# Six shared chunks instead of seven ahead of the routed experts, and the weights' low halves on POOL

## The reference

```python
x = x + 0.5 * ffn(layernorm(x))          # layer half 0
x = x + attention(layernorm(x))
x = x + 0.5 * ffn(layernorm(x))          # layer half 1, same weights

def ffn(h):                              # 8 routed experts, F = 512, the best 2 of 8 per token
    probs = softmax(h @ gate_W.T)
    gates = the two largest of probs, 0 for the others
    out_e = (silu(h @ w1_e[e]) * (h @ w3_e[e])) @ w2_e[e]
    routed = sum over e of gates[e] * out_e
    shared = (silu(h @ w1_s) * (h @ w3_s)) @ w2_s / 8     # 8 shared parts of 64, together 512 wide
    return 0.5 * shared + 0.5 * routed

def attention(a):                        # linear: exp(k) weights, cumulative sums over the sequence
    q, k, v = split(rms_norm(a) @ w_qkv.T)
    w = exp(rms_norm(k))
    y = sigmoid(rms_norm(q)) * cumsum(w * v) / (cumsum(w) + 1e-6)
    u, g = split(y @ w_swiglu.T)
    return a + (u * silu(g)) @ w_out.T
```

## Time and profile before

| what | value |
|---|---|
| median of 3 runs | 734.16 us (734.12 to 734.52) |
| span of the profiled execution | 733.5 us, 0.7 us below the median |
| PE busy | 660.3 us, 90% of the span |
| DVE busy | 458.8 us, 63% |
| ACT busy | 411.3 us, 56% |
| POOL busy | 430.6 us, 59% |
| routed stage of half 0 | 112.4 to 302.1 us |
| attention's first DVE instruction | 313.1 us |

### The profile page before, as it was taken

The page is one execution under the profiler, slowest core; times in us unless marked ns, Lnnn a source line. Parts: engine busy times, 40 slices in busy tenths (PEclk is TensorE's granted clock), DMA queues, the critical chain, the costliest instruction groups (busy, mean ns, idle before and its releaser), DMA issues.

```text
span 733.5 us, 14294 instructions
## 1 busy us (share of the span) xinstructions
PE 660.3 (90%) x4860; PEld 602.1 (82%) x4860; DVE 458.8 (63%) x1177; ACT 411.3 (56%) x861; POOL 430.6 (59%) x511
## 2 busy tenths in 40 slices
PE   3878999999999999957987777999999999999995
PEld 3767879999999999825654574888999999999983
DVE  6678895554445555359999867884555555544536
ACT  2658617666666666236654436664666666666520
POOL 5600075777777776489987424007577777777530
PEclk9989999999999999989999997999999999999999
DMA  9542011221222231131100002402212212212137
GB/s 296 231 78 40 1 42 38 56 52 52 52 55 52 52 53 44 57 105 44 47 12 1 0 1 46 73 2 49 40 55 54 52 52 56 51 53 52 43 104 261
DMA packets 35685, 45.91 MB, mean 63 GB/s; under 512 B 6432, under 2 KB 27936, under 8 KB 35232
## 3 DMA queue, kind: packets, MB, share of 16 engines
q1 hardware_dynamic: 25632, 24.39, 11.8%
q0 software_dynamic: 9984, 20.63, 11.5%
HBM read 28.41 MB, written 16.58 MB: 61 GB/s over the span
## 4 chain that ended last, share of the span: by engine, by line
PE 65%; DVE 20%; issue 4%; ACT 4%; POOL 3%; DMA 2%; SPq 1%; ACTq 0%; POOLq 0%; DVEq 0%
PE psY L1487 18%; PE psG L1334 6%; PE psU L1336 6%; PE psG L1336 6%; PE psU L1335 6%; PE psG L1335 6%; PE psU L1334 6%; PE psH L1405 4%; DVE rec L1076 3%; PE psT L1433 2%; DVE hs L748 2%; DVE XN L738 2%; DVE ln_stats L725 1%; DVE xn L1060 1%; POOL results L641 1%
## 5 line engine op out<-in xcount | busy, mean ns | idle before, releaser
L626 POOL DMA_INDIRECT rows<-tokens,source x156 | 153.7, 985 | 156.3 <-DVE source L900 98.6
L1155 ACT ACTIVATE silu<-psG 128x512 f32<-128x512 f32 x220 | 131.1, 596 | 150.6 <-PE psG L1336 147.2
L954 DVE TENSOR_TENSOR hT<-silu,psU 128x512 f32<-128x512 f32 x156 | 107.4, 688 | 158.9 <-PE psU L1336 150.3
L641 POOL DMA_INDIRECT results<-yout,target x156 | 153.8, 986 | 63.3 <-issue 45.7
L1487 PE MATMUL psY<-W,hT 128*128 x1232 | 162.4, 275 | 1.8 <-DVE yout L980 1.8
L1487 PEld LDWEIGHTS psY<-W,hT 128*128 128x128 f32 x1232 | 150.4, 191 | 2.2 <-DVE hT L954 2.2
L1229 ACT ACTIVATE w_high<-W13H 128x1024 fp32r x78 | 82.7, 1061 | 59.0 <-PE psU L1336 54.8
L1334 PE MATMUL psG<-xTH,w_high 128*128 128x256 f32 x312 | 100.0, 321 | 0.7 <-ACT w_low L1229 0.7
L1336 PE MATMUL psG<-xTH,w_low 128*128 128x256 f32 x312 | 88.0, 282 | 0.0
L1336 PE MATMUL psU<-xTH,w_low 128*128 128x256 f32 x312 | 88.0, 282 | 0.0
L1335 PE MATMUL psU<-xTL,w_high 128*128 128x256 f32 x312 | 87.7, 281 | 0.0
(11 more groups left out here) (188 smaller groups left out, 1215.7 us busy)
## 6 DMA issues: line engine op xcount, KB each, us to landing
W<-w_e SPq DMA_DIRECT2D x3, 2048.0 KB, 13.7
tokens<-XN SPq DMA_DIRECT2D x16, 260.0 KB, 5.9
Y<-results SPq DMA_DIRECT2D x32, 128.0 KB, 2.2
YF<-results SPq DMA_DIRECT2D x16, 256.0 KB, 5.9
rows<-tokens,source POOLq DMA_INDIRECT x156
results<-yout,target POOLq DMA_INDIRECT x156, 2.3
X<-x SPq DMA_DIRECT2D x8, 256.0 KB, 5.5
out<-X SPq DMA_DIRECT2D x8, 256.0 KB, 2.8
```

The costliest lines, as they stand in the source:

```text
L626: pool.indirect_dma_start(rows[:, slot(l, g), t, :], None, tokens, bass.IndirectOffsetOnAxis(ap=source[:, tile:tile + 1], axis=0))\
L641: pool.indirect_dma_start(results, bass.IndirectOffsetOnAxis(ap=target[:, tile:tile + 1], axis=0), yout[:, g % 2, t, :], None).then_inc(y_ ...
L954: dve.tensor_tensor(hT[:, s.u // PT % 2, half, :].rearrange("p f c -> p (f c)"), silu[:, s.u % 2, :], psU[:, s.u % 2, :], ALU.mult).then_i ...
L1155: act.activation(silu[:, s.u % 2, :], psG[:, s.u % 2, :], ACT.Silu).then_inc(silu_done, 1)
```

## The change

Two constants change: `FRONT` is [6, 6], and the seventh chunk (number 6) is `LATE_CHUNK`. Its four steps, its `out_shared` and its `add_shared` stand behind the routed stage in both halves; in half 1 they did so before. Its hidden values go to `hs_late`, a tile of its own that lies over the routing's `at_place`, `in_tile` and `pair`, since `Y` covers the half of `hs` that it had. The 8 `low_part` calls leave DVE's queue. POOL makes them right behind the tokens' low parts, ahead of its wait for the tables and the first `fetch_row`, each as soon as ACT has made its high piece. DVE's copy of the first group of rows (`copy_xT`) and PE's turning of it follow `FRONT` and stand four steps earlier.

```diff
-FRONT = [7, 6]
+FRONT = [6, 6]
+LATE_CHUNK = 6
...
         memory = overlaid(
+            [("below_late", [P, 2 * FT * CH * P], fp32), ("hs_late", [P, FT, CH * P], fp32)],
             [("Y", [P, 4, TOPK, TB, D], fp32), ("XNT", [P, NT], fp32)],
...
 # POOL, behind low_xnT and low_shared
+                def low_part(j):
+                    w, cols = j % 2, bass.ds(j // 2 * WCOLS, WCOLS)
+                    pool.wait_ge(high_made, j + 1)
+                    pool.tensor_tensor(W13L[:, w, cols], W13[:, w, cols], W13H[:, w, cols].bitcast(fp32),
+                                       ALU.subtract).then_inc(w_split, 1)
+                if l == 0:
+                    for j in range(2 * WPARTS):
+                        low_part(j)
                 pool.wait_ge(tokens_out, 16 * CHUNKS * (l + 1))
...
 # DVE
-                    gated(hs[:, s.u // FT, s.u % FT, :], s, shared_at(l, s.i))
+                    home = hs_late if s.i // FT == LATE_CHUNK else hs[:, s.u // FT, :, :]
+                    gated(home[:, s.u % FT, :], s, shared_at(l, s.i))
...
-                def low_part(j):
-                    w, cols = j % 2, bass.ds(j // 2 * WCOLS, WCOLS)
-                    dve.wait_ge(high_made, j + 1)
-                    dve.tensor_tensor(W13L[:, w, cols], W13[:, w, cols], W13H[:, w, cols].bitcast(fp32),
-                                      ALU.subtract).then_inc(w_split, 1)
...
-                    if l == 0 and 0 < k - TABLE_STEP[0] <= 2 * WPARTS:
-                        low_part(k - TABLE_STEP[0] - 1)
...
                 for k in range(front[0], SHARED):
                     gated_shared(Step.of(k, 2 * FT))
+                    if k % FT == 6 % FT and k // FT > FRONT[0]:
+                        add_shared(k // FT - 1)
...
 # PE, out_shared
-                            i = pe.matmul(psH[:, par, t * D:(t + 1) * D], hs[:, par, f, t * P:(t + 1) * P],
+                            i = pe.matmul(psH[:, par, t * D:(t + 1) * D], home[:, f, t * P:(t + 1) * P],
```

More of the change, by code:

```diff
@@ L299, in macaron @@
         hs = memory["hs"]
+        hs_late = memory["hs_late"]
         silu = memory["silu"]
@@ L1402, in out_shared @@
                         pe.wait_ge(sh_added, c + (CHUNKS * l - 1))
+                    home = hs_late if c == LATE_CHUNK else hs[:, par, :, :]
                     for t in range(CH):
                         for f in range(FT):
-                            i = pe.matmul(psH[:, par, t * D:(t + 1) * D], hs[:, par, f, t * P:(t + 1) * P],
+                            i = pe.matmul(psH[:, par, t * D:(t + 1) * D], home[:, f, t * P:(t + 1) * P],
                                           W2S[:, f, :], start=(f == 0), stop=(f == FT - 1))
```

## The result

The changed kernel takes 748.34 us (median of 4 runs, 747.12 to 748.57) beside 734.34 us for the kernel before on the same chip (4 runs, 734.12 to 735.35): ratio 1.0186, 95% interval 1.0172 to 1.0199. It is 14.0 us slower; 744.3 was forecast.

What follows compares the result with a forecast made beforehand. Routing batches on DVE and ACT were taken to pace half 0's front, with PE waiting, though PE leads elsewhere. +11 - 10.1 + 9.0 + 0.8 - 0.6 = +10.1 on 733.5, plus 0.7: 744.3 us; own range 742 to 747, whole 739.5 to 748.5.

Steps and rivals of the forecast that it cites:

- the rival with the larger slip: Front: PE's clock stays at 0.84 and below, slip 13 to 15, POOL's lag costs its full 1.4; 748 us; chance 0.10.
- POOL's lag: Routed stage: POOL's gathers lead PE by less, so PE waits for a buffer; +0.8 us, between 0 and 1.4.
- slip of the front by stalls: Half 0's front: DVE instructions stand while POOL subtracts, so the tables come later; +11 us taken, 12.0 counted.
- start against the first gather: Front's end, DVE not slowed: routed stage starts at 102.3 instead of 112.42, the first gather at 91.97; -10.1 us.
- chunk 6 at the seam: Seam to the attention: four `in_shared` steps and one `out_shared` now stand behind the routed stage; +9.0 us.
- L1047 and the additions: Seam: POOL's first two result additions are done long before, so L1047 no longer meets the second; -0.6 us.
- The seven that were counted: Front: DVE's waits at POOL's pieces 0 to 6, from `onehot` through `slots_of` to the batches; 12.8 us in all.
- The eighth: Front: piece 7 meets a batch beside an `out_shared`, where DVE waits for PE anyway; no cost.
- the rival by which only fp32 forms wait: Front: bf16 batches and integer steps pass POOL; slip 7.2 to 9.5, total 740.5 to 742.8 us; chance 0.24.
- Off the path: Front: DVE's stalls fill its idle time or POOL waits instead; 733.3 us, no measurable change; chance 0.08.
- faster: Front opens at 102.3, subtractions over before `slots_of`, and no buffer wait comes; 732.5 us; chance 0.05.
- The signs named ahead: New profile: L796 2.1 us, ranking 48, DVE excess 13 to 15, first gather 103, routed start 113.3, first L1047 324.

Runs made afterwards that it cites:

- run 3: Kernel before plus eight POOL subtractions of the change's size that nothing needs, in half 0 ahead of the tables; 748.32 us, one run.
- run 2: Kernel before with only the late chunk: six chunks ahead, low halves still on DVE behind the tables; 745.93 us, ratio 1.0152.
- run 6: Kernel before with the late chunk and the low halves on DVE in steps where it waits anyway, none on POOL; 736.18 us, ratio 1.0013.
- run 8: Changed kernel with each of POOL's eight subtractions cut into two of half the columns; 746.39 us, ratio 1.0168 against the kernel before.
- run 10: As run 6, with PE's output products ahead of the transposes in half 0 only; 737.54 us, ratio 1.0036 against the kernel before.
- run 7: Changed kernel with PE's output products ahead of the transposes in both halves; 751.18 us, ratio 1.0226 against the kernel before.
- run 1: Kernel before with only the low halves moved to POOL, seven chunks still ahead; 746.00 us, ratio 1.0150.
- run 5: Kernel before with the eight low-half subtractions on DVE in steps where it waits for PE anyway, seven chunks ahead; 732.52 us, ratio 0.9969.

## Why the prediction was right, and what it mis-sized

The forecast was slower by 10.1 us on the span and 744.3 us; the mechanism, its place and its sign hold. The size doesn't: 748.34 lies outside the forecast's own range of 742 to 747, and only 0.2 us inside the upper end of the whole range, 748.5. That it lies inside at all is partly luck, since 1.1 us were given back behind `at_rstd` that no term had reckoned with. It is the number of the rival with the larger slip (748), though by another sum: the slip came out in its 13 to 15, POOL's lag cost nothing instead of its full 1.4, and the start, which that rival took over unchanged, gave back 2.5 us too little. At `at_rstd` the terms compare so (last column from the milestones):

| step | predicted | measured |
|---|---|---|
| slip of the front by stalls | +11 (12.0 counted) | +13.56 |
| start against the first gather | -10.1 | -7.63 |
| chunk 6 at the seam | +9.0 | +9.08 |
| POOL's lag in the routed stage | +0.8 | -0.22 |
| L1047 and the additions | -0.6 | -0.72 |
| sum at `at_rstd` | +10.1 | +14.07 |

**The stalls.** The seven that were counted (1.7, 1.1, 2.2, 2.0, 1.7, 1.9, 2.2: 12.8) measured 12.5, hit by hit within 0.3. The eighth was taken to fall into idle time and measured 2.13: the slip of the seven before had moved it onto an `in_tile` that DVE had to run. And the +11 taken instead of the counted 12.0 leaned to rows of before that showed no cast, scan, integer or bf16 form beside POOL. All four wait: 2.12, 2.10, 1.15, 1.60 us. That rules out the rival by which only fp32 forms wait, and run 3 shows both bf16 forms waiting without any of the change. "Off the path" and "faster" fall with the first gather.

**The start.** This step had no term for PE's clock. It was to come 10.3 us behind the first gather and came 12.8. The rows are there 7.20 us after the first gather (105.53 to 112.73), where 6.0 was reckoned (91.97 to 98.0): they land 3.2 us behind the start of the fourth gather, not the 2.23 of a scatter. Then the wait of 2.77 us cost the clock: from the rows to the start are 5.62 us, not 4.3. The prediction looked for a fallen clock behind the ranking alone. It fell there (0.63 in 43 to 50 us, 0.67 before) and twice more in the front (0.50 in 60 to 64 us and in 76 to 80, at waits of PE for DVE's work of 5.82 and 2.51 us), but that hardly cost anything: DVE led there, and its idle time up to the first gather didn't grow (8.5 us, 9.4 before). Runs 2, 6, 8 and 10 show the fall behind waits of 3.08, 3.06, 2.09 and 2.38 us, and run 7, which fills the wait, keeps 1.00 in half 0.

**The seam.** From the last `yout` to the last addition are 19.28 us in the changed kernel and in runs 2 and 6, which have the late chunk, and 10.19 to 10.20 us in the kernel before and in runs 1, 3 and 5, which don't. The difference, 9.08 to 9.09, is the term as reckoned.

**POOL's lag.** The wait of `yout` for its buffer didn't come. The later start against the first gather gave POOL 2.5 us back, more than the 1.4 it was reckoned to lack: at group 5's first gather (131.04) POOL waits 0.61 us for PE's side instead of coming late. The stage takes 189.49 us, 189.71 before.

**Around the span.** 0.7 us was added, the distance of the profiled span to the median. The timed runs have their own spans, and there the distance is 1.7 to 1.8 us in each. The profiled execution of before was thus a long one, by 1 us; that is why the medians are 14.0 apart and the spans 13.0. Of the 14.07 at `at_rstd`, 1.1 is gone by the end in parts that nothing edited, within their variation shown above.

**The signs named ahead.** L796, now L810, takes 2.04 us (2.1 named), the ranking comes at 48.09 (48), the excess on DVE is 14.6 us (13 to 15). The first gather is at 105.53 (103), the routed start at 118.35 (113.3), the first `at_var` at 328.52 (324). A routed start much later than 10.5 us behind the first gather was to mean a wait on the rows or the weights: it comes 12.82 behind, and the wait is the one for the rows, 2.77 us, with the slow clock behind it.

The change asks for 13.6 us of stalls to take 9.8 us of subtractions off a stretch in which, as run 5 shows, 2.3 us could be had from them without POOL. The chunk order by itself costs 3.4 us (run 6 against run 5).

## What to carry to other kernels

An idle engine is not free to use: before moving work to POOL, look up which DVE instructions will run beside it, and count up to one whole POOL instruction for each that it meets (here 1.15 to 2.13 us of 2.34), more so where they form the chain that everything waits for. Look first for gaps on the engine that has the work now; here they gave 0.3% where the move cost 1.5%. When work ahead of a wait is taken out, price what PE does while it stands and at which clock it goes on.

## What the runs showed of the hardware that was not expected

- POOL's gathers wait for DVE too. In run 2 a gather at 93.25 takes 1.39 us instead of 0.94; a subtraction of DVE is on from 92.60 to 93.74, and the excess of 0.45 is about what was left of it. The one at 94.95 (1.43) meets the subtraction that ends at 95.47. The gather that starts with one, at 96.68, takes 0.94. The Trainium skill ("SBUF — State Buffer", Who interferes with whom) infers that a `tensor_tensor` does not hold descriptor generation up; here the gather's instruction is held. Which part of it waits, the making of the descriptors or something else in it, the profile doesn't show.
- PE's granted clock was at 0.50 behind single waits of 2.09 to 3.08 us, after long full-clock work, and stayed there for 2 to 4 us. In run 7 a wait of 1.90 us in half 0 left it at 1.00, and one of 1.89 us in half 1 didn't. Ahead of the first routed product in the kernel before, waits of 1.37 and 0.70 us left it at 1.00.
- Finer pieces on POOL leave the sum of DVE's stalls nearly as it was (13.9 against 14.6 us), since each instruction of a chain of short ones meets a piece of its own.
